# An LSTM step with its gates reordered and two gates packed in half-width products, six softmax heads moved to ScalarE, and a product lag of 4 tiles for 5

## The chip, the cores and the metric

The kernel runs on one core of one Trainium2 chip. The metric is the time of one execution on the device in microseconds, as a median of runs. The core's engines are TensorE (PE in the profile, with PEld for its weight loads), VectorE (DVE), ScalarE (ACT), GpSimd (POOL) and SyncE (SP, which issues DMAs). Each has its own instruction queue, and they meet through semaphores.

## The reference, cut to what matters

Four layers in a row, over an x of 4 x 1024 x 256 in float32. Most of the time goes to the first, a recurrence over 1024 time steps that can't be parallelised over time:

```python
def step(carry, x_t):
    h0, c0, h1, c1, a = carry
    xin = concatenate([x_t, a])
    h0, c0 = lstm_cell(xin, h0, c0, Wi0, Wh0, bi0, bh0)
    h1, c1 = lstm_cell(h0, h1, c1, Wi1, Wh1, bi1, bh1)
    q = h1 @ Wq.T
    attn = softmax(einsum('bh,bsh->bs', q, context))
    mixed = einsum('bs,bsh->bh', attn, context)
    a2 = tanh(concatenate([mixed, h1]) @ Wo.T + bo)
def lstm_cell(x, h, c, ...):      # gates i, f, g, o
    c2 = sigmoid(f) * c + sigmoid(i) * tanh(g)
    h2 = sigmoid(o) * tanh(c2)
```

After it come a quantized feed-forward layer (`gelu(x_q @ W_in_q + b_in)`, hidden width 1024), a cross-attention with 16 heads over 64 keys (`softmax(logits + mask) * group_prob @ v`), and a feed-forward layer with 8 experts. Batch is 4, the width is 256.

## The kernel before

`scan` runs the recurrence. A gate has 256 outputs. They are spread over 4 column strips of the PE array (`j`) with 64 outputs each, and the 256 inputs are cut in two (`k`), so that a gate of one product is 8 matmuls: the state (128 x 4 batch entries) is the stationary operand, 64 columns of weights are moved. A float32 matmul shows in the trace as 2 records, so a gate is 16 records and a product of four gates 64. `product(layer, state, weight, gates, done)` issues them; each layer has three PSUM banks, `F`, `IG` (gates i and g share one, in different rows) and `O`. A step has five such products: `wa` (the fed-back a, which opens the step), `wh1`, `wi1` (on the new h0), `wh0`, `wx`. It has three smaller ones too, `head_product`.

When the last product of a bank is done (`gates_summed`), DVE transposes the bank's 128x64 in blocks of 32x32 (`turn`), ACT takes tanh of it, and DVE computes 2c with one `tensor_tensor_scan` over three entries per state: it needs tanh i and tanh g, and the forget term (1 + tanh f) * c, which a separate DVE instruction (L577) makes first. Then ACT takes tanh of c (L438), keeps c (L439), and DVE makes the new h (L583), on which the next product waits. Engines take their instructions in the order in which `step` writes them.

`ffn_hidden` and `attention` run in tiles of 128 tokens with `in_steps(eng, [(stage, lag), ...])`: at step t the engine executes each stage of the list for tile t - lag, in the order of the list. In `ffn_hidden` PE runs `turn` (transposes a tile) at lag 0 and `products` at lag 5. A group is 4 tiles, whose split copies lie in `parts`, which has two buffers; ACT's `split` for a group waits until all products of the group two before are done. In `attention` (32 tiles) DVE adds the mask, takes the maximum per head, subtracts it, sums the exponentials and adds the output; ACT takes one exponential over 128x1024; GpSimd weighs; PE turns, scores, mixes and projects.

Of the kernel before, what the change touches and what calls it, by code (L numbers as in the profile page):

```python
# [12 lines left out]
AX = mybir.AxisListType  # L13
# [242 lines left out]
def scan(nc, ins, xT_all, a_hist, xres, ffn, w_out_scratch, slots_x, a_rows, w):  # L256

    U = 2
    with ExitStack() as ctx:
# [6 lines left out]
        FIRST = (B, B, 0, B)  # L266
        layer_sums = [m.psum(f"sums{l}", (P, 3, 512)) for l in range(2)]
# [3 lines left out]
        gates_of = [[turned[l][g].rearrange("p (k u) -> p k u", k=2) for g in range(3)] for l in range(2)]  # L271
        a_sumT = a_sum[:, 128:192]
# [7 lines left out]
        c = [m.sbuf(f"c{l}", [P, 2 * B]) for l in range(2)]  # L280
        forget_term = [t[:, 1].rearrange("p k b e -> p (k b) e")[:, :, 2] for t in scanned]
        ig_terms = [t[:, 0].rearrange("p k b e -> p k e b")[:, :, 1:3, :] for t in scanned]
        tanh_f = [m.sbuf(f"tanh_f{l}", [P, 2, B]) for l in range(2)]
# [12 lines left out]
        f_tanh, c_terms, c_done, c_kept, h_factors, h_ready = ([m.sem(f"{n}{l}") for l in range(2)]  # L296
                                                               for n in ("f_tanh", "c_terms", "c_done", "c_kept", "h_factors", "h_ready"))
# [20 lines left out]
        with nc.Block() as block:  # L318
# [99 lines left out]
            def _(act):  # L418
# [9 lines left out]
                def step(n):  # L428
                    for l in range(2):
                        act.wait_ge(gates_turned[l][F], n)  # L430
                        nc.scalar.activation(tanh_f[l][:], gates_of[l][F][:, :, 0:B], ACT.Tanh).then_inc(f_tanh[l], 1)  # L431
                        act.wait_ge(gates_turned[l][IG], n)
                        nc.scalar.activation(ig_terms[l], gates_of[l][IG][:, :, 0:2 * B].rearrange("p k (f b) -> p k f b", f=2),  # L433
                                             ACT.Tanh).then_inc(c_terms[l], 1)
                        act.wait_ge(gates_turned[l][O], n)
                        nc.scalar.activation(tanh_o[l][:], gates_of[l][O][:, :, 0:B], ACT.Tanh).then_inc(h_factors[l], 1)
# [1280 lines left out]
```

## Time and profile before

| | |
|---|---|
| median of 3 runs | 8204.93 us (8202.91 to 8206.75) |
| the profiled execution's own time | 8210.56 us |
| its span | 8208.8 us |
| mean granted TensorE clock | 0.984 |
| busy: PE / PEld / DVE / ACT / POOL | 85% / 72% / 55% / 42% / 4% |

The time is a little more than the span (from first to last instruction). Busy shares are means over stages with different limits. Rows of the trace name the line in the kernel, the engine, and the tiles as output<-input; `scan_sums` are the gate banks.

### The profile page before, as it was taken

The numbers are of one execution on the slowest core, as the hardware profiler recorded it, in microseconds if no ns is written. First come the engines' busy times: TensorE is split into PE (matmuls) and PEld (weight loads), VectorE is DVE, ScalarE is ACT, GpSimd is POOL, SyncE is SP. The second block draws the span as 40 slices with busy tenths as digits, with TensorE's granted clock in tenths as the row PEclk, the third lists the DMA queues.
The fourth block names the chain that finished last, engine by engine and source line by source line (L and its number), as shares of the span: only waits on it lengthen the run. The fifth ranks groups of instructions, "written<-read, shape, count | busy, mean of one in ns | idle before, by whom it ended". The sixth has DMA issues, their size and how long they took to land. (4 is left out here: it accounts for less than half of the span.)

```text
span 8208.8 us, 834179 instructions
## 1 busy us (share of the span) xinstructions
PE 6973.1 (85%) x388633; PEld 5941.0 (72%) x388641; DVE 4544.6 (55%) x21134; ACT 3446.1 (42%) x17105; POOL 312.4 (4%) x332
## 2 busy tenths in 40 slices
PE   7888888888888888888888888888888888868769
PEld 5777777777777777777777777777777777746546
DVE  5555555555555555555555555555555555566822
ACT  3444444444444444444444444444444444452422
POOL 0000000000000000000000000000000000002632
PEclk8999999999999999999999999999999999989889
DMA  3000000000000000000000000000000000000143
GB/s 113 5 0 0 5 0 0 0 0 5 0 0 0 5 0 0 0 0 5 0 0 0 5 0 0 0 5 0 0 0 0 5 0 0 0 14 11 62 148 109
DMA packets 94637, 101.99 MB, mean 12 GB/s; under 512 B 46570, under 2 KB 81904, under 8 KB 93424
## 3 DMA queue, kind: packets, MB, share of 16 engines
q1 hardware_dynamic: 89200, 88.73, 3.6%
q0 software_dynamic: 5376, 12.63, 0.4%
q14 instruction: 45, 0.37, 0.0%
q8 instruction: 16, 0.26, 0.0%
HBM read 79.75 MB, written 23.67 MB: 13 GB/s over the span
## 5 line engine op out<-in xcount | busy, mean ns | idle before, releaser
L361 PE MATMUL scan_sums<-rec_wh,scan_hT 128*4 128x64 f32 x131008 | 2394.5, 219 | 1.4 <-issue 1.3
L492 DVE STREAM_TRANSPOSE scan_sums<-scan_sums 128x64 f32<-128x64 f32 x6144 | 1551.8, 265 | 1129.8 <-PE scan_sums L361 1114.0
L361 PEld LDWEIGHTS scan_sums<-rec_wh,scan_hT 128*4 128x4 f32 x131008 | 1991.4, 89 | 2.2 <-issue 2.1
L361 PE MATMUL scan_sums<-rec_wa,scan_aT 128*4 128x64 f32 (+1 forms) x65536 | 1104.7, 219 | 474.6 <-ACT scan_aT L447 473.7
L361 PEld LDWEIGHTS scan_sums<-rec_wa,scan_aT 128*4 128x4 f32 (+1 forms) x65536 | 915.4, 88 | 663.7 <-ACT scan_aT L447 662.3
L361 PE MATMUL scan_sums<-rec_wx,scan_xT 128*4 128x64 f32 (+1 forms) x65536 | 1291.5, 219 | 3.4 <-issue 2.4
L361 PE MATMUL scan_sums<-rec_wi,scan_hT 128*4 128x64 f32 (+1 forms) x65536 | 1104.2, 219 | 145.0 <-issue 4.5
L361 PEld LDWEIGHTS scan_sums<-rec_wi,scan_hT 128*4 128x4 f32 (+1 forms) x65536 | 914.4, 88 | 334.5 <-DVE scan_hT L583 328.9
L361 PEld LDWEIGHTS scan_sums<-rec_wx,scan_xT 128*4 128x4 f32 (+1 forms) x65536 | 1023.9, 89 | 4.1 <-issue 2.9
L431 ACT ACTIVATE scan_tanh_f<-scan_sums 128x8 f32<-128x8 f32 x2048 | 364.1, 178 | 1185.9 <-DVE scan_sums L492 1185.8
L426 ACT ACTIVATE scan_sums<-rec_bias 128x192 f32<-128x192 f32 x2050 | 686.7, 335 | 303.9 <-PE scan_sums L408 6.1
L447 ACT ACTIVATE scan_aT<-scan_a_sum 128x8 f32<-128x8 f32 x1024 | 182.0, 178 | 1457.5 <-DVE scan_a_sum L598 1455.3
L372 PE MATMUL scan_scores<-rec_kp,scan_hT 128*4 128x64 f32 x16384 | 416.6, 219 | 372.6 <-DVE scan_hT L583 372.6
L372 PEld LDWEIGHTS scan_scores<-rec_kp,scan_hT 128*4 128x4 f32 x16384 | 227.6, 85 | 558.1 <-DVE scan_hT L583 558.1
L433 ACT ACTIVATE scan_scanned<-scan_sums 128x16 f32<-128x16 f32 x2048 | 393.0, 192 | 517.6 <-DVE scan_sums L492 502.1
L583 DVE SCALAR_TENSOR_TENSOR scan_hT<-scan_tanh_o,scan_sums 128x8 f32<-128x8 f32 x2048 | 335.9, 164 | 466.5 <-ACT scan_sums L438 466.0
L587 DVE TENSOR_REDUCE scan_neg_max<-scan_scores 128x1 f32<-128x65 f32 x1024 | 231.4, 226 | 517.4 <-PE scan_scores L372 517.4
L442 ACT ACTIVATE scan_exps<-scan_scores,scan_neg_max 128x64 f32<-128x64 f32 x1024 | 321.5, 314 | 430.9 <-DVE scan_neg_max L587 430.1
L581 DVE TENSOR_TENSOR_SCAN scan_sums<-scan_scanned 128x24 f32<-128x24 f32 x2048 | 443.6, 217 | 62.6 <-ACT scan_scanned L433 0.2
L372 PE MATMUL scan_a_sum<-rec_woh,scan_hT 128*4 128x64 f32 x16384 | 416.5, 219 | 0.0
L372 PE MATMUL scan_scores<-rec_vp,scan_expsT 128*4 128x64 f32 x16384 | 416.5, 219 | 0.0
L596 DVE SCALAR_TENSOR_TENSOR scan_a_natural<-scan_scores,scan_inv,scan_from_h 128x64 f32<-128x64 f32 x1024 | 290.8, 284 | 222.3 <-PE scan_scores L372 222.2
(265 smaller groups left out, 6480.6 us busy)
## 6 DMA issues: line engine op xcount, KB each, us to landing
experts_bias<-in_b SPq DMA_DIRECT2D x40, 640.0 KB, 4.3
moe_w<-in_w SPq DMA_DIRECT2D x16, 1024.0 KB, 14.7
slots_x<-scan_blank SPq DMA_DIRECT2D x40, 129.0 KB
experts_x<-slots_x SPq DMA_DIRECT2D x40, 129.0 KB
w_xres<-in_x_steps SPq DMA_DIRECT2D x8, 512.0 KB, 7.3
w_xres<-in_x SPq DMA_DIRECT2D x4, 1024.0 KB, 12.2
x_rows<-w_xres SPq DMA_DIRECT2D x4, 1024.0 KB, 8.5
a_rows<-scan_stage SPq DMA_DIRECT2D x224, 16.0 KB, 1.5
```

The costliest lines, as they stand in the source:

```text
L361: last = nc.tensor.matmul(sums[layer][BANK[g]][32 * j:32 * j + ROWS[g], 0:64], state[:, k, FIRST[g]:FIRST[g] + ROWS[g]], weight[:, k, j, 6 ...
L372: last = nc.tensor.matmul(bank[32 * j:32 * j + B, 0:64], state[:, k, :], weight[:, k, j, :], start=k == 0, stop=k == 1, skip_group_check=True)
L426: nc.scalar.activation(layer_sums[l][:, :, 0:64], w["bias"][:, l, :, :], ACT.Copy).then_inc(seeded[l], 1)
L431: nc.scalar.activation(tanh_f[l][:], gates_of[l][F][:, :, 0:B], ACT.Tanh).then_inc(f_tanh[l], 1)
L433: nc.scalar.activation(ig_terms[l], gates_of[l][IG][:, :, 0:2 * B].rearrange("p k (f b) -> p k f b", f=2), ACT.Tanh).then_inc(c_terms[l], 1)
L442: nc.scalar.activation(exps[:], scores[:, 0:S], ACT.Exp, bias=neg_max[:], accum_out=total[:]).then_inc(exps_done, 1)
L447: nc.scalar.activation(state_of(aT), a_sumT.rearrange("p (k u) -> p k u", k=2)[:, :, 0:B], ACT.Tanh).then_inc(a_ready, 1)
L492: nc.vector.transpose(turned[l][g], sums[l][g][:, 0:64]).then_inc(gates_turned[l][g], 1)
L581: nc.vector.tensor_tensor_scan(cell[l], flat[l][:, 0], flat[l][:, 1], 0.0, ALU.mult, ALU.add).then_inc(c_done[l], 1)
L583: nc.vector.scalar_tensor_tensor(state_of(hT[l]), tanh_o[l][:], 1.0, tanh_c[l].rearrange("p (k b) -> p k b", k=2), ALU.add, ALU.mult).then ...
L587: nc.vector.tensor_reduce(neg_max[:], scores[:, 0:S + 1], AX.X, ALU.max, negate=True).then_inc(max_done, 1)
L596: nc.vector.scalar_tensor_tensor(a_natural[:], mixed, inv[:], from_h[:], ALU.mult, ALU.add).then_inc(a_scaled, 1)
```

## The change

It has three parts.

1. In `scan` the gates are issued in the order i, g, f, o. Gates f and o, which used 4 rows of 64 columns, now use 8 rows of 32: each matmul of 64 columns becomes two of 32, one for each half of the strip's outputs, both summed in the same 32 columns, with the state at another row offset. DVE turns 128x32 for these two. The bias rows are laid out to match. On DVE the separate instruction now makes (1 + tanh i) * tanh g; c goes straight into the scan's operand (written there by ACT), and tanh f is written there too. The scan over three entries stays.
2. In `ffn_hidden` PE's `products` follow at lag 4.
3. In `attention` the first 6 heads (`LONE`) are taken by ACT in 6 instructions, each with the negated maximum as bias and the sum of the exponentials in `accum_out`. DVE subtracts and sums for the other 10 heads. ACT's order is turned copies, lone heads, mixed copy, exponential of the other 10. PE's next scores wait for the lone heads of the tile two before.

```diff
-                def product(layer, state, weight, gates=(GATE_F, GATE_I, GATE_G, GATE_O), done=None):
+                def product(layer, state, weight, gates=(GATE_I, GATE_G, GATE_F, GATE_O), done=None):
                     for g in gates:
-                        for k in range(2):
-                            for j in range(4):
-                                last = nc.tensor.matmul(sums[layer][BANK[g]][32 * j:32 * j + ROWS[g], 0:64],
-                                                        state[:, k, FIRST[g]:FIRST[g] + ROWS[g]],
-                                                        weight[:, k, j, 64 * g:64 * g + 64], start=False,
+                        packed = g in HALVED
+                        for half in range(2 if packed else 1):
+                            first, rows = (B * (1 - half), 2 * B) if packed else (FIRST[g], ROWS[g])
+                            width = 32 if packed else 64
+                            for k in range(2):
+                                for j in range(4):
+                                    last = nc.tensor.matmul(sums[layer][BANK[g]][32 * j:32 * j + rows, 0:width],
+                                                            state[:, k, first:first + rows],
+                                                            weight[:, k, j, 64 * g + 32 * half:64 * g + 32 * half + width], start=False,
...
                     for l in range(2):
+                        act.wait_ge(gates_turned[l][IG], n)
+                        nc.scalar.activation(tanh_ig[l][:], gates_of[l][IG][:, :, 0:2 * B].rearrange("p k (f b) -> p f k b", f=2),
+                                             ACT.Tanh).then_inc(ig_tanh[l], 1)
                         act.wait_ge(gates_turned[l][F], n)
-                        nc.scalar.activation(tanh_f[l][:], gates_of[l][F][:, :, 0:B], ACT.Tanh).then_inc(f_tanh[l], 1)
-                        act.wait_ge(gates_turned[l][IG], n)
-                        nc.scalar.activation(ig_terms[l], gates_of[l][IG][:, :, 0:2 * B].rearrange("p k (f b) -> p k f b", f=2),
-                                             ACT.Tanh).then_inc(c_terms[l], 1)
+                        nc.scalar.activation(f_factor[l], halved_of(l, F), ACT.Tanh).then_inc(c_terms[l], 1)
...
-                        nc.scalar.activation(c[l][:], twice_c[l], ACT.Copy, scale=0.5).then_inc(c_kept[l], 1)
+                        nc.scalar.activation(c_factor[l], twice_c[l], ACT.Copy, scale=0.5).then_inc(c_kept[l], 1)
...
-                    nc.vector.transpose(turned[l][g], sums[l][g][:, 0:64]).then_inc(gates_turned[l][g], 1)
+                    width = 32 if g in (F, O) else 64
+                    nc.vector.transpose(turned[l][g][:, 0:width], sums[l][g][:, 0:width]).then_inc(gates_turned[l][g], 1)
...
+                        turn(l, IG, n)
                         turn(l, F, n)
-                        turn(l, IG, n)
-                        dve.wait_ge(f_tanh[l], n)
-                        nc.vector.scalar_tensor_tensor(forget_term[l], tanh_f[l][:].rearrange("p k b -> p (k b)"), 1.0, c[l][:],
+                        dve.wait_ge(ig_tanh[l], n)
+                        nc.vector.scalar_tensor_tensor(input_term[l], tanh_ig[l][:, 0].rearrange("p k b -> p (k b)"), 1.0,
+                                                       tanh_ig[l][:, 1].rearrange("p k b -> p (k b)"),
                                                        ALU.add, ALU.mult).then_inc(c_terms[l], 1)
...
-                in_steps(pe, [(turn, 0), (products, 5)], NB // 2, 2 * B)
+                in_steps(pe, [(turn, 0), (products, 4)], NB // 2, 2 * B)
...
-                    pe.wait_ge(shifted, number(g, b))
+                    pe.wait_ge(lone_done, LONE * number(g, b))
...
+                def lone_exps(g, b):
+                    act.wait_ge(shifted, number(g, b) + 2)
+                    for h in range(LONE):
+                        nc.scalar.activation(probs[b % 2][:, h, :], heads_of[b % 2][:, h, :], ACT.Exp, bias=neg_high[b % 2][:, h:h + 1],
+                                             accum_out=total[b % 2][:, h:h + 1]).then_inc(lone_done, 1)
+
                 def exps(g, b):
-                    act.wait_ge(shifted, number(g, b) + 2)
-                    nc.scalar.activation(probs[b % 2][:], probs[b % 2][:], ACT.Exp).then_inc(exp_done, 1)
+                    nc.scalar.activation(probs[b % 2][:, LONE:H, :], probs[b % 2][:, LONE:H, :], ACT.Exp).then_inc(exp_done, 1)
...
-                in_steps(act, [(fetch, 0), (keep_turned, 3), (exps, 1), (keep_mixed, 3)])
+                in_steps(act, [(fetch, 0), (keep_turned, 3), (lone_exps, 1), (keep_mixed, 3), (exps, 1)])
...
-                    nc.vector.tensor_tensor(probs[s][:], heads_of[s], high[s][:].unsqueeze(2).broadcast_to([P, H, S]),
-                                            ALU.subtract).then_inc(shifted, 1)
+                    nc.vector.tensor_tensor(probs[s][:, LONE:H, :], heads_of[s][:, LONE:H, :],
+                                            neg_high[s][:, LONE:H].unsqueeze(2).broadcast_to([P, H - LONE, S]), ALU.add).then_inc(shifted, 1)
...
-                    nc.vector.tensor_reduce(total[b % 2][:], probs[b % 2][:], AX.X, ALU.add).then_inc(total_done, 1)
+                    nc.vector.tensor_reduce(total[b % 2][:, LONE:H], probs[b % 2][:, LONE:H, :], AX.X, ALU.add).then_inc(total_done, 1)
```

PE at the start of a time step, before: product `wa` on the fed-back a (4 or 8 stationary columns, 64 moved, xN matmuls).

```order
L361 MATMUL scan_sums<-rec_wa,scan_aT 4x64 [waits scan_a_ready]
L361 MATMUL scan_sums<-rec_wa,scan_aT 4x64 x7
L361 MATMUL scan_sums<-rec_wa,scan_aT 8x64 x16
L361 MATMUL scan_sums<-rec_wa,scan_aT 4x64 x8
L361 MATMUL scan_sums<-rec_wh,scan_hT 4x64 [waits scan_seeded1]
```

The same place in the change:

```order
L367 MATMUL scan_sums<-rec_wa,scan_aT 8x64 [waits scan_a_ready]
L367 MATMUL scan_sums<-rec_wa,scan_aT 8x64 x15
L367 MATMUL scan_sums<-rec_wa,scan_aT 8x32 x32
L367 MATMUL scan_sums<-rec_wh,scan_hT 8x64 [waits scan_seeded1]
```

Gates i and g come first, and the 8 + 8 matmuls of f and o have become 16 + 16 of half the width: 48 for 32.

DVE in one LSTM cell of layer 0, before, where `summed_f0` and its like are the PE's signals:

```order
L492 STREAM_TRANSPOSE scan_sums<-scan_sums 128x64 [waits scan_summed_f0]
L492 STREAM_TRANSPOSE scan_sums<-scan_sums 128x64 [waits scan_summed_ig0]
L577 SCALAR_TENSOR_TENSOR scan_scanned<-scan_tanh_f,scan_c 128x8 [waits scan_f_tanh0]
L492 STREAM_TRANSPOSE scan_sums<-scan_sums 128x64 [waits scan_summed_o0]
L581 SCALAR_TENSOR_TENSOR scan_sums<-scan_scanned 128x24 [waits scan_c_terms0]
```

And in the change:

```order
L499 STREAM_TRANSPOSE scan_sums<-scan_sums 128x64 [waits scan_summed_ig0]
L499 STREAM_TRANSPOSE scan_sums<-scan_sums 128x32 [waits scan_summed_f0]
L584 SCALAR_TENSOR_TENSOR scan_scanned<-scan_tanh_ig 128x8 [waits scan_ig_tanh0]
L499 STREAM_TRANSPOSE scan_sums<-scan_sums 128x32 [waits scan_summed_o0]
L589 SCALAR_TENSOR_TENSOR scan_sums<-scan_scanned 128x24 [waits scan_c_terms0]
```

The transposes have changed places, f's and o's are half as wide, and the small instruction ahead of o's transpose now waits for the tanh of i and g.

ACT in one tile of `attention` in the change, in the unrolled end of the stage (before, the two rows of L1165 were one, of 128x1024, and nothing stood behind the mixed copy):

```order
L1176 ACTIVATE ffn_hidden<-attn_turned 128x512 [waits attn_turned_done,attn_mixed_done]
L1176 ACTIVATE ffn_hidden<-attn_turned 128x512 [waits attn_turned_done]
L1165 ACTIVATE ffn_hidden<-attn_scores,ffn_hidden 128x64 [waits attn_shifted]
L1165 ACTIVATE ffn_hidden<-attn_scores,ffn_hidden 128x64 x5
L1181 ACTIVATE ffn_hidden<-attn_mixed 128x256 [waits attn_mixed_done]
L1169 ACTIVATE ffn_hidden<-ffn_hidden 128x640
```

The large exponential has become six small ones ahead of the mixed copy and a smaller one behind it.

## Rows read from the trace of the kernel before

**Rows 1.** Busy time by engine in two stretches: the scan, and the attention.

```profile
92.00:7250.00 7158.00, 6170.52 (x383986) 5394.95 (x383973) 3985.87 (x19667) 3070.14 (x16341) 20.64 (x56) 1.00 0.01 1
...
7534.00:7722.00 188.00, 138.67 (x887) 77.86 (x886) 160.90 (x184) 82.31 (x143) 124.79 (x83) 0.94 0.00 0
```

**Rows 2.** Timeline of one step: start us, duration us, engine, line, [idle before].

```profile
4001.86 1.08 PE L361 MATMUL scan_sums<-rec_wa,scan_aT 128*4 128x64 f32 x64 [0.46 <-ACT scan_aT L447]
...
4002.78 0.27 DVE L492 STREAM_TRANSPOSE scan_sums<-scan_sums 128x64 f32<-128x64 f32 x1 [0.16 <-PE scan_sums L361]
...
4002.96 0.15 DVE L577 SCALAR_TENSOR_TENSOR scan_scanned<-scan_tanh_f,scan_c 128x8 f32<-128x8 f32 x1
4003.01 0.27 DVE L492 STREAM_TRANSPOSE scan_sums<-scan_sums 128x64 f32<-128x64 f32 x1
4003.08 0.19 ACT L433 ACTIVATE scan_scanned<-scan_sums 128x16 f32<-128x16 f32 x1 [0.25 <-DVE scan_sums L492]
4003.31 0.18 ACT L436 ACTIVATE scan_tanh_o<-scan_sums 128x8 f32<-128x8 f32 x1
4003.31 0.22 DVE L581 TENSOR_TENSOR_SCAN scan_sums<-scan_scanned 128x24 f32<-128x24 f32 x1
4003.56 0.16 ACT L438 ACTIVATE scan_sums<-scan_sums 128x8 f32<-128x8 f32 x1
...
4003.97 1.08 PE L361 MATMUL scan_sums<-rec_wi,scan_hT 128*4 128x64 f32 x64
...
4008.86 0.35 PE L361 MATMUL scan_sums<-rec_wa,scan_aT 128*4 128x64 f32 x12 [0.46 <-ACT scan_aT L447]
```

**Rows 3.** Groups by shape from 3000 to 4000 us: xcount | busy us, mean ns.

```profile
L492 DVE STREAM_TRANSPOSE scan_sums<-scan_sums 128x64 f32<-128x64 f32 x858 | 215.8, 266 | 155.9 <-PE scan_sums L361 155.9
...
L591 DVE STREAM_TRANSPOSE scan_expsT<-scan_exps 128x64 f32<-128x64 f32 x142 | 34.8, 245 | 35.5 <-ACT scan_exps L442 35.5
...
L398 PE MATMUL scan_a_sum<-scan_total,w_ident 128*4 128x1 f32 x1136 | 30.6, 166 | 0.0
...
L533 DVE STREAM_TRANSPOSE scan_stage<-scan_part 128x128 f32<-128x128 f32 x8 | 2.5, 312 | 1.4 <-POOL scan_part L327 1.4
```

**Rows 4.** Timeline: ScalarE's one exponential with a sum in the scan.

```profile
4006.81 0.31 ACT L442 ACTIVATE scan_exps<-scan_scores,scan_neg_max 128x64 f32<-128x64 f32 x1 [0.42 <-DVE scan_neg_max L587]
4007.02 0.19 ACT L442 ACTIVATION_READ_ACCUMULATOR scan_exps<-scan_scores,scan_neg_max 128x1 f32 x1
```

**Rows 5.** Timeline of one attention tile: DVE, then PE, then ACT.

```profile
7604.70 1.22 DVE L1177 TENSOR_TENSOR attn_scores<-attn_scores,ffn_hidden 128x1024 f32<-128x1024 f32 x1
...
7610.36 1.22 DVE L1177 TENSOR_TENSOR attn_scores<-attn_scores,ffn_hidden 128x1024 f32<-128x1024 f32 x1
...
7606.51 1.09 PE L1118 MATMUL attn_turned<-w_ident,ffn_hidden 128*128 128x128 f32 x8 [0.47 <-POOL ffn_hidden L1216]
...
7610.59 1.10 PE L1137 MATMUL attn_y<-ffn_wo,ffn_hidden 128*128 128x256 f32 x4 [0.70 <-DVE w_xres L1198]
...
7607.20 1.09 ACT L1160 ACTIVATE ffn_hidden<-attn_turned 128x512 f32<-128x512 f32 x2 [2.35 <-PE attn_turned L1118]
...
7609.96 0.39 ACT L1165 ACTIVATE ffn_hidden<-attn_mixed 128x256 f32<-128x256 f32 x1 [0.36 <-PE attn_mixed L1128]
```

**Rows 6.** Groups by shape from 7440 to 7790 us: DVE over 1024 and 512 elements.

```profile
L1183 DVE TENSOR_TENSOR ffn_hidden<-attn_scores,ffn_hidden 128x1024 f32<-128x1024 f32 x32 | 39.2, 1225 | 3.3
...
L1060 DVE TENSOR_TENSOR ffn_hidden<-ffn_hidden 128x512 f32<-128x512 f32 x8 | 4.9, 686 | 6.0 <-ACT ffn_hidden L1019 6.0
```

**Rows 7.** PE's waits from 7280 to 7375 us: total us, times, longest.

```profile
PE hidden_turned L801 <- DVE hidden_xq L846: 21.8, 18, 1.6
```

**Rows 8.** Timeline of the hidden stage: two of PE's transposes, and a split on ACT.

```profile
7302.25 0.44 PE L801 MATMUL hidden_turned<-w_ident,hidden_xq 128*128 128x128 f32 x2 [1.61 <-DVE hidden_xq L846]
...
7313.08 0.44 PE L801 MATMUL hidden_turned<-w_ident,hidden_xq 128*128 128x128 f32 x2 [1.60 <-DVE hidden_xq L846]
...
7311.59 0.38 ACT L825 ACTIVATE hidden_parts<-hidden_turned 128x256 bf16<-128x256 f32 x1 [1.35 <-PE hidden_summed L811]
```

More of the change, by code:

```diff
@@ L279, in scan @@
         twice_c = [t.rearrange("p (v e) -> p v e", e=3)[:, :, 2] for t in cell]
[L280 to L283, printed above, removed]
+        input_term = [t[:, 1].rearrange("p k b e -> p (k b) e")[:, :, 2] for t in scanned]
+        f_factor = [t[:, 0, :, :, 1] for t in scanned]
+        c_factor = [t[:, 0].rearrange("p k b e -> p (k b) e")[:, :, 2] for t in scanned]
+        tanh_ig = [m.sbuf(f"tanh_ig{l}", [P, 2, 2, B]) for l in range(2)]
         tanh_o = [m.sbuf(f"tanh_o{l}", [P, 2, B]) for l in range(2)]
@@ L295, in scan @@
         gates_turned = [[m.sem(f"turned_{g}{l}") for g in ("f", "ig", "o")] for l in range(2)]
-        f_tanh, c_terms, c_done, c_kept, h_factors, h_ready = ([m.sem(f"{n}{l}") for l in range(2)]
-                                                               for n in ("f_tanh", "c_terms", "c_done", "c_kept", "h_factors", "h_ready"))
+        ig_tanh, c_terms, c_done, c_kept, h_factors, h_ready = ([m.sem(f"{n}{l}") for l in range(2)]
+                                                               for n in ("ig_tanh", "c_terms", "c_done", "c_kept", "h_factors", "h_ready"))
         (a_ready, x_ready, scores_done, max_done, exps_done, exps_turned, h_summed, h_kept, total_spread, a_terms, a_scaled, a_turned,
@@ L355, in _ @@
             def _(pe):
-                def product(layer, state, weight, gates=(GATE_F, GATE_I, GATE_G, GATE_O), done=None):
+                def product(layer, state, weight, gates=(GATE_I, GATE_G, GATE_F, GATE_O), done=None):
                     for g in gates:
-                        for k in range(2):
-                            for j in range(4):
-                                last = nc.tensor.matmul(sums[layer][BANK[g]][32 * j:32 * j + ROWS[g], 0:64],
-                                                        state[:, k, FIRST[g]:FIRST[g] + ROWS[g]],
-                                                        weight[:, k, j, 64 * g:64 * g + 64], start=False,
-                                                        stop=done is not None and g != GATE_I and k == 1, skip_group_check=True)
+                        packed = g in HALVED
[7 more added lines that the diff above has]
+                                                            weight[:, k, j, 64 * g + 32 * half:64 * g + 32 * half + width], start=False,
+                                                            stop=done is not None and g != GATE_I and k == 1 and (half == 1 or not packed),
+                                                            skip_group_check=True)
                         if done is not None and g != GATE_I:
@@ L1084, in attention @@
         mixedT = [m.sbuf(f"mixedT{i}", [P, KC, P]) for i in range(2)]
-        high, total, inv = (([m.sbuf(f"{n}{i}", [P, H]) for i in range(2)]) for n in ("high", "total", "inv"))
+        LONE = 6
+        neg_high, total, inv = (([m.sbuf(f"{n}{i}", [P, H]) for i in range(2)]) for n in ("neg_high", "total", "inv"))
         scores = [m.psum(f"scores{i}", (P, KC, 512)) for i in range(2)]
@@ L1669, in bias_rows @@
         rows = np.zeros((4, 32, GATES, 64), bias.dtype)
-        for g, first in enumerate((0, 0, B, 0)):
-            rows[:, first:first + B, g, :] = gate_blocks(bias)[g][:, None, :]
+        blocks = gate_blocks(bias)
+        for g, first in ((1, 0), (2, B)):
+            rows[:, first:first + B, g, :] = blocks[g][:, None, :]
+        for g in (0, 3):
+            for half in range(2):
+                rows[:, B * half:B * half + B, g, 0:32] = blocks[g][:, None, 32 * half:32 * half + 32]
         return rows.reshape(P, GATES, 64)
```

11 lines of the change are left out of this document (7 added, 4 removed).

## The prediction, made before the changed kernel was run

> **What bounds the kernel now.** I read the busy time by stretches first: the scan takes 7158 of 8209 us [rows 1], so a change of 0.01 us in a time step is worth 10 us. PE is busy 86% of it, which looks like the bound, but the timeline of one step says otherwise. A step lasts 7.00 us (4001.86 to 4008.86), and PE opens it after 0.46 us of waiting for `scan_aT` [rows 2]. The end is set by a ring of short dependent instructions: PE, transpose, tanh, scan, tanh, h, PE, twice per step, and then the attention part. PE's other products fill its waits.
>
> Follow cell 0 [rows 2]. PE starts `wa` at 4001.86. The transpose of bank IG starts at 4002.78, 0.92 after it, and takes 0.266 us [rows 3]. ACT's tanh of IG runs 4003.08 to 4003.27, the scan starts at 4003.31, tanh of c at 4003.56, the next product at 4003.97. The reader is to see that IG, the second bank, is on the path, and that o's transpose (4003.01 to 4003.28) ends at almost the same moment, so both have to get earlier. From the start of `wa` to the scan it is 1.45 us.
>
> **The scan, part by part.** First the pitch of PE. The 64 records of `wa` last 1.08 us and one lasts 0.219, so the starts spread over 0.861 us [rows 2] (one with a single column lasts 0.166 [rows 3]). The four column strips run side by side, so this is 16 groups of 4 records. I take 0.02 us for the starts within a group and get (0.861 - 0.02) / 15 = 0.056 us from group to group. What a group of 32 columns needs, no row shows. Bounds: if only the columns count, 0.028. If nothing is saved, 0.056. The nearest row is the spread of totals with one column, 8 records (2 groups): 1136 records are 142 steps, 30.6 / 142 = 0.2155 us each, less 0.166 is 0.0495, less 0.02 leaves 0.03 for the second group [rows 3]. I take 0.031, as 32 columns can't be quicker than one, and call it P.
>
> The end of a matmul moves too: 64 columns take 0.219, one takes 0.166 [rows 2, 3], so 32 take about 0.192, 0.027 less.
>
> Path through the second bank, now f: before, the last group of IG started 11 x 0.056 = 0.613 after the first and the transpose 0.92 after it, an offset of 0.307. Now it is 8 x 0.056 + 7 x 0.031 = 0.663, and 0.663 + 0.307 - 0.027 = 0.943. The transpose is 128x32. From 64 to 128 columns it goes from 0.245 to 0.312 us [rows 3], so 32 columns less are 0.033 less: 0.233. Handing over to ACT takes 0.03 (4003.05 to 4003.08), tanh over 8 elements 0.178 where 16 took 0.19 (rows of 4003.31 and 4003.08), and handing over to DVE 0.03 to 0.04 [rows 2]. Sum: 0.943 + 0.233 + 0.033 + 0.178 + 0.032 = 1.42, where the same sum for IG gives 0.92 + 0.266 + 0.033 + 0.19 + 0.032 = 1.44. **0.026 us less.**
>
> Path through the new wait of DVE on `ig_tanh`: behind it on DVE stand o's transpose and the scan. IG now is summed after 7 groups: 0.92 - 0.613 + 0.39 = 0.70; + 0.266 + 0.033 + 0.19 + 0.032 = 1.22 for the small instruction; o's transpose can start 0.05 later (4002.96 to 4003.01), and behind a transpose of 64 columns the next instruction starts 0.18 later (4002.78 to 4002.96) [rows 2], so behind 32 about 0.14: the scan at 1.41. That is just under the other path. Bank O is summed for 0.448 + 15 x 0.031 + 0.28 = 1.19, before 1.27: not late. tanh of o ends at 1.27 + 0.23 + 0.03 + 0.18 = 1.71, before tanh of c would (1.42 + 0.22 + 0.03 + 0.16 = 1.83): hidden. With P = 0.028 the f path gives 1.40 and DVE's 1.41 decides: 0.034 us less. With P = 0.0347 the gain is nil (0.026 / 7 more). Both cells are alike (`wi1` starts at 4003.97 after the same ring), so a step gains 0.052 us: **53 us** over 1024 steps (70 at P = 0.028).
>
> PE's load: a product takes 8 x 0.056 + 16 x 0.031 = 0.94 where it took 0.89. `wa` and `wh1` end at 4001.86 + 1.88 = 4003.74, ahead of 4003.97: hidden. The exponential is read out at 4007.21 [rows 4] while PE, delayed by two packed gates (0.05), finishes about there. It costs nothing, and without that cover up to 0.05 us a step (50 us). ACT's copy of c and the seeds only write elsewhere: nothing.
>
> **Attention.** One tile takes 5.66 us (7604.70 to 7610.36) [rows 5], and DVE is busy 161 of the stage's 188 us [rows 1]. 1024 elements take 1.225 us, 512 take 0.686 [rows 6]: 1.05 ns an element. Subtraction and sum each lose 384: 0.40 us each, so DVE would allow 4.86. But a new ring appears: PE turns, ACT copies 0.69 later (7606.51 to 7607.20), two copies 0.99, six heads, mixed copy 0.39, PE projects (1.10, of which 0.87 until the next can start) and turns the next tile [rows 5], since the mixed copy now stands behind the lone heads. A head: the read of the sum starts 0.21 behind the exponential and lasts 0.19 [rows 4]. Bounds 0.28 and 0.40 a head; I take 0.34, as ACT's instructions overlap by some 0.1 us. Ring: 0.69 + 0.99 + 6 x 0.34 + 0.39 + 0.06 + 0.87 = 5.04 us. The tile gains 0.62 (0.26 at 0.40 a head, 0.80 at 0.28 where DVE decides). Times 31 tiles: **19 us** (8 to 25).
>
> **Hidden stage.** A group of 4 tiles takes 10.83 us (7302.25 to 7313.08), and PE waits 1.6 us in each at one tile, where ACT's split waits for PE's products of the group two before [rows 8]. With lag 5 these stand behind the turn of the tile that needs the buffer. With lag 4 they stand ahead of it, so that wait goes. The stage has 8 groups; six such waits are 10 us. All 18 waits add up to 21.8 us [rows 7], of which 12 lie in the start, where the products now begin one tile sooner, and in shorter waits behind the long one. Of these I take a third: **14 us** in all (8 to 16). The products need the tile whose low part DVE made before the turn ahead of them: no new wait.
>
> **Sum.** 53 + 19 + 14 = 86 us of the profiled 8210.6: 8124.6. The median of the runs is 5.6 us lower than that execution, so 8204.9 - 86 = 8119 us.
>
> **A rule of the skill against it.** The spread shows four matmuls of one column started in about 0.05 us [rows 3], 0.013 each, and a float32 matmul of 64 columns now costs 0.056 / 2 = 0.028 of PE's time. The Trainium skill, TensorE: Matmul & The Clock Gate, section "Wait — 56ns, not 53.3ns?", says that start-to-start never drops below about 25 ns, however few columns. By that rule a matmul of 32 columns would save next to nothing, and rival 2 would be the result. The one-column row speaks against it across strips, but it is a burst of four behind a wait, not a stream of 48.
>
> **Rivals.**
> 1. P is 0.034 to 0.037: the scan gains nothing (8172 by the 33 us of the other stages) or gives back as much as they bring (at 0.037, 0.0023 x 7 x 2048 = 33 us, 8205). For it: the P of the one-column row comes from two groups with 4 stationary columns, not 8. Chance 0.14.
> 2. Slower: issue sets PE's pace, not columns. Its place is f and o in `wa` and `wi1`, its price for P = 0.050 (a matmul no cheaper than 0.025 us): bank O's last group starts at 0.448 + 15 x 0.05 = 1.20, its transpose at 1.48, the scan at 1.62 to 1.65, 0.2 us later in each cell: 410 us, less 33: 8580. It decides from P = 0.038 on. For it: 188 matmuls a step are now 268. Against it: the one-column row. Chance 0.12.
> 3. More: a transpose of 32 columns takes 0.21 and frees DVE after 0.12, P = 0.028. Then f's path is 1.375 and DVE's 1.39: 0.055 less in each cell, 113 us, with 19 to 40 from the others: 8060. For it: a 128x8 instruction takes only 0.15 [rows 2]. Chance 0.14.
>
> **Chances and range.** The forecast, 8119, 0.60 (its own range 8090 to 8160). A measurement of this kernel tells 0.2%, 16 us, from no change. Faster: 0.60 + 0.14 + half of rival 1, less 0.02 for what I don't see: 0.79. Within 0.2%: 0.08. Slower: 0.13. Rival 2 stays outside, as do the ends of the others: 8052 to 8208.
>
> **What would show it.** In the profile after: the groups of 128x32 matmuls, whose 32 records per gate spread over 8P (0.25 us; 0.40 means rival 2); the transpose of f at 0.94 after `wa` starts, of 0.23 us; the scan at 1.42; steps of 6.95 us; PE's waits on `scan_aT` still there. In attention DVE's add every 5.0 us with PE's projection waiting on ACT's mixed copy. In the hidden stage groups of 8.7 to 9.3 us. It is wrong if a strip's weight load with 8 stationary columns can't be renewed in 0.03 us, or if two halves that add to the same PSUM columns hold each other up.

## The result

The changed kernel took 8238.53 us (median of 5 runs, 8236.22 to 8241.55), the kernel before 8204.93 (8202.25 to 8207.31, 5 runs beside them): a ratio of 1.004, interval 1.0027 to 1.0054. It is slower by 34 us where 86 less were forecast. Two of the three parts brought what was forecast or more; the third, which carried most of the sum, has the wrong sign.

The page of the kernel after: span, busy time of TensorE (PE) and of its weight loads (PEld), and the granted clock in 40 slices.

```profile
span 8234.5 us, 1162182 instructions
...
PE 7411.6 (90%) x552448; PEld 6680.3 (81%) x552449; DVE 4494.4 (55%) x21132; ACT 3459.2 (42%) x17489; POOL 312.4 (4%) x332
...
PEclk8999999999999999999999999999999999999889
```

Before, the same page has 388633 records of PE in 6973.1 us. So 42% more matmul records, and PE busy for 438 us more. The clock row differs in one slice alone, behind the scan (9 where 8 stood before), and in the scan the granted clock is 1.00 in both kernels: the 2.4 GHz level, so the scan's difference doesn't come from there.

Busy time by engine in the scan of the kernel after (stretch, length, then each engine's busy time and records; to be set beside [rows 1]).

```profile
92.00:7317.00 7225.00, 6621.45 (x547637) 6138.50 (x547629) 3964.58 (x19675) 3048.89 (x16346) 20.57 (x56) 1.00 0.01 1
```

Where the time went is read from the first start of one line in each stage, before and after:

| first start of | before | after | shift |
|---|---|---|---|
| the scan's products | 61.5 | 59.9 | -1.6 |
| (last `wh` product of the scan) | 7247.5 | 7314.8 | +67.3 |
| hidden stage, turning | 7278.8 | 7346.8 | +68.0 |
| `output_summed` | 7386.2 | 7440.0 | +53.8 |
| attention, DVE's add | 7560.8 | 7613.9 | +53.1 |
| routing, turning | 7759.6 | 7786.3 | +26.7 |
| end of the span | 8208.8 | 8234.5 | +25.7 |

The scan lost 69 us, the hidden stage gave back 14 and attention 26. (Between the spans lie 26 us, between the medians 34.)

One time step of the kernel after, in the timeline (start us, duration us; to be set beside [rows 2]).

```profile
4004.68 1.20 PE L367 MATMUL scan_sums<-rec_wa,scan_aT 128*8 128x64 f32 x96 [0.42 <-ACT scan_aT L454]
...
4005.38 0.53 DVE L499 STREAM_TRANSPOSE scan_sums<-scan_sums 128x64 f32<-128x64 f32 x2 [0.44 <-PE scan_sums L367]
4005.68 0.19 ACT L438 ACTIVATE scan_tanh_ig<-scan_sums 128x16 f32<-128x16 f32 x1 [0.85 <-DVE scan_sums L499]
...
4005.70 1.17 PE L367 MATMUL scan_sums<-rec_wh,scan_hT 128*8 128x64 f32 x96
4005.90 0.17 DVE L584 SCALAR_TENSOR_TENSOR scan_scanned<-scan_tanh_ig 128x8 f32<-128x8 f32 x1
4005.94 0.18 ACT L441 ACTIVATE scan_scanned<-scan_sums 128x8 f32<-128x8 f32 x1
4005.99 0.23 DVE L499 STREAM_TRANSPOSE scan_sums<-scan_sums 128x32 f32<-128x32 f32 x1
4006.16 0.22 DVE L589 TENSOR_TENSOR_SCAN scan_sums<-scan_scanned 128x24 f32<-128x24 f32 x1
...
4006.41 0.16 ACT L445 ACTIVATE scan_sums<-scan_sums 128x8 f32<-128x8 f32 x1
...
4006.82 1.20 PE L367 MATMUL scan_sums<-rec_wi,scan_hT 128*8 128x64 f32 x96
```

The two transposes in one row are IG's (64 columns) and f's (32); f's takes the last 0.23 of the 0.53, so it starts at 4005.68, 1.00 after `wa`, where 0.94 was forecast. ACT's tanh of f (L441) starts at 4005.94, 0.26 later, and the scan at 4006.16: 1.48 after `wa`, where 1.42 was forecast and 1.45 was read before. The 96 records of `wa` last 1.20 us and one of 32 columns 0.193 (below), so the starts spread over 1.01 us where 0.93 was forecast (0.913 to the last group and 0.02 within it).

Groups by shape of the kernel after from 3000 to 4000 us (busy us, mean ns; to be set beside [rows 3]).

```profile
L367 PE MATMUL scan_sums<-rec_wa,scan_aT 128*8 128x32 f32 x9088 | 106.1, 193 | 0.0
...
L499 DVE STREAM_TRANSPOSE scan_sums<-scan_sums 128x32 f32<-128x32 f32 x566 | 129.0, 228 | 7.7
...
L367 PE MATMUL scan_sums<-rec_wa,scan_aT 128*8 128x64 f32 x4544 | 89.9, 219 | 59.4 <-ACT scan_aT L454 59.4
L499 DVE STREAM_TRANSPOSE scan_sums<-scan_sums 128x64 f32<-128x64 f32 x283 | 75.1, 265 | 167.3 <-PE scan_sums L367 167.3
...
L584 DVE SCALAR_TENSOR_TENSOR scan_scanned<-scan_tanh_ig 128x8 f32<-128x8 f32 x283 | 48.8, 172 | 0.2 <-ACT scan_tanh_ig L438 0.2
```

The durations of single instructions were forecast well: 0.193 for 0.192, 0.228 for 0.233. What was not is how closely the matmuls follow each other.

The starts of the single records of `wa` show it (ns; 230 is the first one; two records a matmul, eight to a line). In every step from 3000 to 3800 us the closely spaced starts end at the same record, the first of the 13th matmul.

```
after, gate g, last lines (64 columns)     569  575  582  589   625  631  638  645
after, gate f (2 x 32 columns)             680  687  694  700   709  715  722  729
                                           738  745  751  758   767  774  780  787
                                           796  803  810  816   825  832  839  845
                                           855  879  884  895   909  912  925  946
after, gate o                              955  971  985  988  1001 1005 1017 1021 ... 1217 1239
16-column kernel (e5), gate f              679  686  693  700   708  715  721  728
                                           733  740  747  753   759  765  771  779
                                           783  790  797  804   809  815  822  829
                                           834  871  879  895   909  912  924  946
16-column kernel, gate o                   954  971  984  988  1002 1005 1017 1022 ... 1217 1239
```

Groups of four records come every 56 ns with 64 columns. With 32 they come every 29 ns, as forecast, but only from 680 to 855, for 12 matmuls; with 16 every 26 ns, for the same 12. Behind them there is a matmul (two records) every 16.6 ns, with 32 columns and with 16: 33 ns for a group of four. f's last record starts 0.717 us behind the first (a median of 0.716) where 0.683 was forecast (0.663 for the last group and 0.02 within it), o's at 1.009.

### The profile page after: what moved, and what is told of

Read it like the earlier page. It is cut to its first block and busy times, and to the rows that moved or that the text cites. A ratio compares the mean times of both kernels' runs of the same rounds, so it can differ in the third digit from the quotient of the medians.

```text
span 8234.5 us, 1162182 instructions
## 1 busy us (share of the span) xinstructions
PE 7411.6 (90%) x552448; PEld 6680.3 (81%) x552449; DVE 4494.4 (55%) x21132; ACT 3459.2 (42%) x17489; POOL 312.4 (4%) x332
## 5 line engine op out<-in xcount | busy, mean ns | idle before, releaser
L367 PE MATMUL scan_sums<-rec_wh,scan_hT 128*8 128x64 f32 (+1 forms) x196512 | 2640.6, 202 | 7.3 <-issue 7.3
L367 PEld LDWEIGHTS scan_sums<-rec_wh,scan_hT 128*8 128x8 f32 x196512 | 2249.8, 89 | 7.8 <-issue 7.8
L499 DVE STREAM_TRANSPOSE scan_sums<-scan_sums 128x32 f32<-128x32 f32 (+1 forms) x6144 | 1475.2, 240 | 1285.3 <-PE scan_sums L367 1229.3
L367 PE MATMUL scan_sums<-rec_wa,scan_aT 128*8 128x64 f32 (+1 forms) x98304 | 1227.9, 202 | 426.4 <-ACT scan_aT L454 426.2
L367 PEld LDWEIGHTS scan_sums<-rec_wa,scan_aT 128*8 128x8 f32 x98304 | 1095.3, 89 | 557.7 <-ACT scan_aT L454 557.3
L367 PE MATMUL scan_sums<-rec_wx,scan_xT 128*8 128x64 f32 (+1 forms) x98304 | 1416.8, 202 | 3.3 <-issue 2.5
L367 PE MATMUL scan_sums<-rec_wi,scan_hT 128*8 128x64 f32 (+1 forms) x98304 | 1228.2, 202 | 5.7 <-issue 5.3
L367 PEld LDWEIGHTS scan_sums<-rec_wi,scan_hT 128*8 128x8 f32 x98304 | 1095.4, 89 | 88.2 <-issue 5.6
L367 PEld LDWEIGHTS scan_sums<-rec_wx,scan_xT 128*8 128x8 f32 x98304 | 1155.6, 89 | 3.9 <-issue 2.7
L438 ACT ACTIVATE scan_tanh_ig<-scan_sums 128x16 f32<-128x16 f32 x2048 | 377.7, 184 | 1619.8 <-DVE scan_sums L499 1619.8
L441 ACT ACTIVATE scan_scanned<-scan_sums 128x8 f32<-128x8 f32 x2048 | 373.9, 183 | 154.8 <-DVE scan_sums L499 2.2
```

The lines of the kernel that those rows point to most:

```text
L438: nc.scalar.activation(tanh_ig[l][:], gates_of[l][IG][:, :, 0:2 * B].rearrange("p k (f b) -> p f k b", f=2), ACT.Tanh).then_inc(ig_tanh[l], 1)
L441: nc.scalar.activation(f_factor[l], halved_of(l, F), ACT.Tanh).then_inc(c_terms[l], 1)
L499: nc.vector.transpose(turned[l][g][:, 0:width], sums[l][g][:, 0:width]).then_inc(gates_turned[l][g], 1)
```

## The experiments

Times are medians. Of kernels timed in rounds the interval of the ratio is given; the kernel before took 8205.52 beside e1 to e4, 8203.55 beside e5 to e7 and 8205.6 beside e8 to e11. Times within a step are medians over 3000 to 3800 us, counted from the first start of `wa`.

| us after `wa` starts | before | after | e2 | e3 | e4 | e5 | e6 | e7 |
|---|---|---|---|---|---|---|---|---|
| last start of f's matmuls | .188 | .716 | .638 | .638 | .716 | .717 | .717 | .557 |
| transpose of f starts | .474 | .994 | .924 | .924 | .993 | .993 | .994 | .875 |
| tanh ends | 1.412 | 1.441 | 1.405 | 1.405 | 1.439 | 1.439 | 1.441 | 1.308 |
| transpose of o starts | 1.144 | 1.301 | 1.300 | 1.300 | 1.299 | 1.300 | 1.300 | 1.299 |
| scan starts | 1.444 | 1.475 | 1.466 | 1.437 | 1.472 | 1.472 | 1.473 | 1.432 |
| scan ends | 1.661 | 1.692 | 1.653 | 1.653 | 1.689 | 1.689 | 1.690 | 1.636 |
| step | 7.000 | 7.067 | 6.989 | 6.988 | 7.058 | 7.058 | 7.066 | 6.955 |

(The tanh is that of i and g in the kernel before, of f in the others. The scan's end is what tanh of c, and so the rest of the ring, waits for.)

**e1, the scan of before with the two other parts.**

```diff
-                def product(layer, state, weight, gates=(GATE_I, GATE_G, GATE_F, GATE_O), done=None):
+                def product(layer, state, weight, gates=(GATE_F, GATE_I, GATE_G, GATE_O), done=None):
...
```

> The scan of the kernel before with the change's hidden and attention stages. By the traces the scan of the changed kernel is 69 us longer (a step 7.067 for 7.000 us), the hidden stage 14 us and the attention 26 us shorter. Theory (all of the loss lies in the scan): 8205 - 41 = 8164 us. Rival (the scan's loss is partly put down wrongly and the later stages gave less): above 8180.

Measured: 8164.9, ratio 0.995 (0.9937 to 0.9964). The attention and hidden parts bring 41 us together; the loss is the scan's alone. The diffs that follow leave out lines that only fit the kernel to the edit (the bias rows, the views of the turned gates).

**e2, the new order of gates without packing.**

```diff
-        HALVED = (GATE_F, GATE_O)
+        HALVED = ()
...
-                    width = 32 if g in (F, O) else 64
+                    width = 64
```

> The change without the packing: gates in the order i, g, f, o, all 64 columns wide, 32 matmuls a product. Theory A (PE can't issue a float32 matmul faster than one in 16.6 ns, so the 32 halves run dry and f and o are summed 0.03 and 0.08 us late): step 6.99 to 7.00 us, 8155 to 8166 us. Theory B (the new order itself costs: DVE's small instruction now waits for tanh of i and g, two transposes stand back to back): the step stays at 7.06 us, 8225 to 8240 us.

Measured: 8151.84, ratio 0.9933 (0.992 to 0.9947), 13 us below e1 and the fastest of the kernels that compute the whole layer (e3's and e10's intervals overlap its own). Its timeline of one step:

```profile
3999.87 1.08 PE L367 MATMUL scan_sums<-rec_wa,scan_aT 128*8 128x64 f32 x64 [0.47 <-ACT scan_aT L454]
...
4000.57 0.49 DVE L499 STREAM_TRANSPOSE scan_sums<-scan_sums 128x64 f32<-128x64 f32 x2 [0.44 <-PE scan_sums L367]
...
4001.09 0.17 DVE L584 SCALAR_TENSOR_TENSOR scan_scanned<-scan_tanh_ig 128x8 f32<-128x8 f32 x1
4001.09 0.18 ACT L441 ACTIVATE scan_scanned<-scan_sums 128x8 f32<-128x8 f32 x1
4001.17 0.26 DVE L499 STREAM_TRANSPOSE scan_sums<-scan_sums 128x64 f32<-128x64 f32 x1
4001.34 0.19 DVE L589 TENSOR_TENSOR_SCAN scan_sums<-scan_scanned 128x24 f32<-128x24 f32 x1
...
4006.86 1.08 PE L367 MATMUL scan_sums<-rec_wa,scan_aT 128*8 128x64 f32 x64 [0.47 <-ACT scan_aT L454]
```

The tanh of f starts at 4001.09, 1.22 after `wa`; with packing it was 1.26. The step is 6.989 for 7.000 before: the order gains 0.011 us a step, 11 of the 13 us, and the theory that the order or its new wait costs the time falls: the loss comes with the packing.

**e3 and e4, only one gate packed.**

```diff
-        HALVED = (GATE_F, GATE_O)
+        HALVED = (GATE_O,)        (e3)
+        HALVED = (GATE_F,)        (e4)
```

> Order i, g, f, o, only o packed. Theory A: f is summed after 12 groups as IG was before; o is summed in time behind the small instruction: scan of a cell 1.44 us after the product starts, step 7.00 us, 8158 to 8170 us. Theory B: 8225 to 8240 us.

> Order i, g, f, o, only f packed. Theory A: f's last matmul is as late as in the changed kernel (0.72 us after the product's start, for 0.63 unpacked), its narrower transpose and shorter matmul give back 0.06 of the 0.08: step 7.05 to 7.06 us, 8220 to 8238 us. If the late o alone is at fault: 8165 us.

Measured: e3 8157.94 (0.9941, 0.9926 to 0.9956), its step 6.988, as in e2; e4 8229.84 (1.003, 1.0019 to 1.0042). Of the 87 us between e2 and the changed kernel, 78 come with f. In e4's timeline:

```profile
4002.39 0.17 DVE L584 SCALAR_TENSOR_TENSOR scan_scanned<-scan_tanh_ig 128x8 f32<-128x8 f32 x1
4002.43 0.18 ACT L441 ACTIVATE scan_scanned<-scan_sums 128x8 f32<-128x8 f32 x1
4002.47 0.26 DVE L499 STREAM_TRANSPOSE scan_sums<-scan_sums 128x64 f32<-128x64 f32 x1
4002.64 0.22 DVE L589 TENSOR_TENSOR_SCAN scan_sums<-scan_scanned 128x24 f32<-128x24 f32 x1
```

Here the small DVE instruction (L584) and o's transpose stand against each other as in e2, but tanh of f starts 0.04 behind the first of them instead of beside it, and the scan follows it. In e3 the scan starts 0.03 earlier than in e2 but is drawn 0.22 long for 0.19: it ends at 1.653 in both, 0.248 behind the end of the tanh of f. So the scan's start is a poor measure, and its end hangs on f; a narrower transpose of o buys nothing. In e3 the burst is seen once more: o's 16 matmuls come behind 24 of 64 columns instead of 16, and again 12 of them come at 14.6 ns each, with a gap of 24 ns behind them. So the burst doesn't get longer with more matmuls ahead of it, and it isn't tied to gate f.

**e5, e6 and e7: why the packed matmuls are slow.** Three kernels vary one thing each in the packed gates of the changed kernel: moved columns, stationary columns (`rows` in the code, 8 or 4), and count. None of them computes the layer: e5 leaves out half of what f and o sum, e6 adds both halves into the same rows, and e7 leaves the second halves out.

```diff
# e5: moved columns
-    sums[layer][BANK[g]][32 * j:32 * j + rows, 0:width]
+    sums[layer][BANK[g]][32 * j:32 * j + rows, 0:width // 2 if packed else width]
...
# e6: stationary columns
-    first, rows = (B * (1 - half), 2 * B) if packed else (FIRST[g], ROWS[g])
+    first, rows = (B, B) if packed else (FIRST[g], ROWS[g])
# e7: count
-    for half in range(2 if packed else 1):
+    for half in range(1):
...
```

> The changed kernel with the packed matmuls cut to 16 moved columns (half of what gates f and o sum is left out); as many matmuls. Theory A (issue): once PE has used up what was issued ahead, one float32 matmul still takes 16.6 ns, so bank O's last matmul starts only 0.0 to 0.05 us earlier than the 1.01 us after wa's first, and a step stays at 7.02 to 7.06 us. Rival C (columns and their turnaround set the pace of the halves): twice as quick, O's last matmul at 0.8 us.

> The changed kernel with 4 stationary columns for 8 in the packed halves (each half then adds into the same rows, so f and o are wrong sums); as many matmuls of 32 columns. Theory A (issue): pace and step unchanged, 16.6 ns and 7.06 us. Rival D (the load of 8 stationary columns can't be renewed in 0.03 us): the pace falls to 14.5 ns or less and the step to 7.03 us or less.

> The changed kernel with the second halves of f and o left out: 32 matmuls a product, half of them of 32 columns. Theory A: f is summed early enough for its transpose to stand right behind IG's, and what is left is DVE's and ACT's own chain through tanh of i and g: scan 1.42 to 1.45 us after wa starts, step 6.96 to 6.99 us. If the step stays above 7.04 the matmuls aren't at fault.

Measured, one run each: 8231.34, 8242.14 and 8122.49. Half the columns change little (a step of 7.058 for 7.067): e5's `wa` and `wh1` still start 1.02 apart, as in the changed kernel (4004.68, 4005.70), and the list of starts above runs into the same times from 879 on.

```profile
4003.72 1.19 PE L367 MATMUL scan_sums<-rec_wa,scan_aT 128*8 128x64 f32 x96 [0.43 <-ACT scan_aT L454]
4004.74 1.15 PE L367 MATMUL scan_sums<-rec_wh,scan_hT 128*8 128x64 f32 x96
4005.86 1.19 PE L367 MATMUL scan_sums<-rec_wi,scan_hT 128*8 128x64 f32 x96
```

In e6 tanh of f stands 1.26 behind `wa` and the scan 1.48, and the starts of `wa` lie within 2 ns of the changed kernel's: the eight stationary columns are not it either.

```profile
4000.95 1.20 PE L367 MATMUL scan_sums<-rec_wa,scan_aT 128*8 128x64 f32 x96 [0.42 <-ACT scan_aT L454]
...
4002.21 0.18 ACT L441 ACTIVATE scan_scanned<-scan_sums 128x8 f32<-128x8 f32 x1
...
4002.43 0.22 DVE L589 TENSOR_TENSOR_SCAN scan_sums<-scan_scanned 128x24 f32<-128x24 f32 x1
```

Only the count moves it. In e7 the packed gates have as many matmuls as unpacked ones, and as many moved columns in all as in e5, where there are twice as many matmuls:

```profile
4002.55 0.91 PE L367 MATMUL scan_sums<-rec_wa,scan_aT 128*8 128x64 f32 x64 [0.57 <-ACT scan_aT L454]
...
4003.67 0.18 ACT L441 ACTIVATE scan_scanned<-scan_sums 128x8 f32<-128x8 f32 x1
4003.76 0.17 DVE L584 SCALAR_TENSOR_TENSOR scan_scanned<-scan_tanh_ig 128x8 f32<-128x8 f32 x1
4003.85 0.23 DVE L499 STREAM_TRANSPOSE scan_sums<-scan_sums 128x32 f32<-128x32 f32 x1
4003.98 0.20 DVE L589 TENSOR_TENSOR_SCAN scan_sums<-scan_scanned 128x24 f32<-128x24 f32 x1
```

It shows a second thing. f is out of the way here (its tanh ends at 1.308), yet the scan starts at 1.432: L584 waits for the tanh of i and g (which ends at 1.18 in every kernel with the new order) and starts at 1.22, the next instruction starts 0.084 behind it and the scan 0.133 behind o's transpose. That is a floor that no speed of f gets under; the forecast had the start at 1.41. The scan ends at 1.636 here, 0.017 before e2's. So 0.034 us a step, 35 us in all, is what a quicker f can still gain on e2 in this order, and this kernel gains it with half of f's and o's work left out.

**e8 and e9, the other two parts alone on the kernel before.**

```diff
# e8
-                in_steps(pe, [(turn, 0), (products, 5)], NB // 2, 2 * B)
+                in_steps(pe, [(turn, 0), (products, 4)], NB // 2, 2 * B)
# e9: the attention part of the change, whole
+        LONE = 6
...
```

> The kernel before with products at lag 4 only. By the traces of before and after the hidden stage (first transpose to the next stage's first product) goes from 107.4 to 93.2 us: 14 us less, 8191 us. Rival: the stages behind hide or give back part of it: 8200 us.

> The kernel before with the new attention only. By the traces the stage (DVE's first add to the next stage's first transpose) goes from 198.8 to 172.4 us: 26 us less, 8179 us.

Measured: 8188.71 (0.9981, 0.9972 to 0.999), 17 us less, and 8179.89 (0.9969, 0.9957 to 0.9981), 26 less. In the changed kernel, PE's waits for the tiles to turn (before, in [rows 7]: 21.8 us, 18 times) and two turns four tiles apart (before, in [rows 8]):

```profile
PE hidden_turned L809 <- DVE hidden_xq L854: 6.7, 5, 1.6
```

```profile
7364.73 0.44 PE L809 MATMUL hidden_turned<-w_ident,hidden_xq 128*128 128x128 f32 x2 [0.34 <-DVE hidden_xq L854]
...
7373.44 0.44 PE L809 MATMUL hidden_turned<-w_ident,hidden_xq 128*128 128x128 f32 x2
```

Four tiles take 8.71 us where they took 10.83. One attention tile of the changed kernel (to be set beside [rows 5]):

```profile
7633.72 1.23 DVE L1193 TENSOR_TENSOR attn_scores<-attn_scores,ffn_hidden 128x1024 f32<-128x1024 f32 x1
...
7634.62 1.13 PE L1148 MATMUL attn_y<-ffn_wo,ffn_hidden 128*128 128x256 f32 x4 [0.51 <-ACT ffn_hidden L1181]
...
7637.20 0.32 ACT L1165 ACTIVATE ffn_hidden<-attn_scores,ffn_hidden 128x64 f32<-128x64 f32 x1
7637.40 0.21 ACT L1165 ACTIVATION_READ_ACCUMULATOR ffn_hidden<-attn_scores,ffn_hidden 128x1 f32 x1
7637.49 0.33 ACT L1165 ACTIVATE ffn_hidden<-attn_scores,ffn_hidden 128x64 f32<-128x64 f32 x1
...
7638.59 1.22 DVE L1193 TENSOR_TENSOR attn_scores<-attn_scores,ffn_hidden 128x1024 f32<-128x1024 f32 x1
```

A head takes 0.29 us (7637.20 to 7637.49): the next exponential starts 0.09 after the read of the sum begins. The tile takes 4.87, and DVE starts its add without a wait: DVE sets it, not the ring.

**e10 and e11, five and seven lone heads, in e2's kernel.**

```diff
-        LONE = 6
+        LONE = 5        (e10)
+        LONE = 7        (e11)
```

> The order without the packing, with 5 lone heads for 6. DVE sets the attention tile (4.87 us with 6 heads; each head back on DVE costs 2 x 64 elements x 1.05 ns = 0.13 us): 5.00 us a tile, 4 us in all slower than the 8152 of 6 heads: 8156 us. If the ring over ACT sets the tile, it gets shorter by 0.29 instead: 8150 us or less.

> The same with 7 lone heads. DVE would allow 4.74 us; the ring PE turns, ACT copies, lone heads at 0.29 us each, mixed copy, PE projects is 0.69 + 0.99 + 7 x 0.29 + 0.39 + 0.06 + 0.87 = 5.03 us: 5 us in all slower, 8157 us. If DVE alone counts: 8148 us.

Measured: 8157.68 (0.9942, 0.9929 to 0.9956) and 8161.31 (0.9947, 0.9933 to 0.9961). Against the kernel before beside each that is 48 and 44 us less, where six heads (e2) gave 54; the intervals overlap. The tiles tell them apart: a median of 4.86 with six, 4.99 with five (DVE has 64 elements more in two instructions), 5.09 with seven, where DVE's add waits for PE's scores. These don't wait themselves: they stand on PE behind the projection (L1148), which waits for ACT's mixed copy (L1181), and that stands on ACT behind the seven lone heads. It is the ring of the prediction, expected at 5.03:

```profile
7609.86 1.23 DVE L1193 TENSOR_TENSOR attn_scores<-attn_scores,ffn_hidden 128x1024 f32<-128x1024 f32 x1 [0.34 <-PE attn_scores L1118]
7614.94 1.23 DVE L1193 TENSOR_TENSOR attn_scores<-attn_scores,ffn_hidden 128x1024 f32<-128x1024 f32 x1 [0.26 <-PE attn_scores L1118]
...
7611.07 1.13 PE L1148 MATMUL attn_y<-ffn_wo,ffn_hidden 128*128 128x256 f32 x4 [0.79 <-ACT ffn_hidden L1181]
7612.03 1.04 PE L1129 MATMUL attn_turned<-w_ident,ffn_hidden 128*128 128x128 f32 x8
7612.91 1.88 PE L1118 MATMUL attn_scores<-ffn_hidden 128*128 128x512 f32 x4
```

The best version is e2: the new order, the hidden and the attention part, and no packing.

## Why the prediction was wrong

**What bounds the kernel: right.** The step is set by the ring of short instructions through the second bank. The scan starts 0.031 us later in each cell (1.475 for 1.444); two cells make 0.062 of the 0.067 us by which the step grew, and 1024 steps make the 69 us. The scan's end moves by as much (1.692 for 1.661). That PE's other products are hidden held too: PE still waits 0.42 us for `scan_aT` before `wa`. The last 0.005 us of the step are not accounted for.

**The pitch P, 0.031: the step that failed.** It was taken from two groups of four records and laid over the 16 groups of gates f and o. The runs show two regimes. A burst comes at the pace of the columns, 0.029 a group at 32, and for that the one-column row was a fair guide. After 12 matmuls the burst is used up, and matmuls start 16.6 ns apart, with 32 columns and with 16 (e5), with eight stationary columns and with four (e6). 0.033 a group is in itself near P, and by the prediction's sum would leave a small gain of about 0.01 us a cell. But the change of regime costs more than the pitches tell: from 855 to 946 there are seven starts, where the burst has some 12. So f's last start came 0.034 late (0.717 for 0.683). That is the larger part of the 0.055 by which the scan started late (1.475 for 1.42).

**The shorter end of a narrower matmul, 0.027: mis-sized.** It was taken from drawn durations (0.219 and 0.192). Behind a last start with 64 columns the transpose follows after 0.287 (0.634 to 0.921 for IG before, and within 0.001 in e2 for f), with 32 columns after 0.277, and with 16 (e5) after 0.277 too. So 0.010 was gained where 0.027 was put, and f's transpose started at 0.994 for 0.943. The other terms of that path (0.233, 0.033, 0.178, 0.032) are right within 0.005 each.

**The sum itself has a slip.** Its own terms give 1.419 for the path through f and 1.441 for the one through IG, 0.022 less and not 0.026: 45 us and not 53. (8 x 0.056 + 7 x 0.031 is 0.665, not 0.663, and 11 x 0.056 is 0.616, not 0.613; these two nearly cancel.)

**The path through the new wait, 1.41: too short by the start, near by the end.** L584 starts at 1.217, as forecast (1.22). What stands behind it starts 0.084 later, where 0.05 was taken from another instruction, so by this path the scan starts at 1.43 (e7: 1.432). But it is drawn 0.204 long there for 0.217 before, and ends at 1.636 for 1.661: 0.025 less in each cell, 51 us. So this path alone would have let most of the forecast through, and e7 shows it: 0.045 us a step less than before.

**What a right pitch would have brought.** The scan ends 0.248 behind the tanh of f in e2, e3 and the changed kernel (within 0.003). With f's starts as forecast its tanh would have ended at 1.441 - 0.034 = 1.407, as in e2, and the scan at 1.655: an estimate of 0.006 a cell, 12 us, and not 53. Had the burst's 0.029 lasted over the whole gate, the last start would be at 0.448 + 7 x 0.029 + 0.02 = 0.671 and the scan's end at 1.643: an estimate of 0.018 a cell, 37 us. No run shows either. What the packing lost against e2 is the pitch; what it could have won was small unless the burst had lasted.

**Bank O in time: wrong in time, harmless.** o's last record starts at 1.009 for 0.933 forecast, but its transpose stands behind L584 on DVE until 1.30 anyway; e3 shows it free.

**Rival 2, issue sets PE's pace:** the mechanism is the one that came, its place and price are not. It put the loss in bank O at 0.2 us a cell (410 us); it lies in f at 0.03. Its floor of 0.050 a group was too high: the groups came every 0.033. The Trainium skill, TensorE: Matmul & The Clock Gate, section "Wait — 56ns, not 53.3ns?", says that start-to-start never drops below about 25 ns. The trace doesn't agree with that figure for matmuls in different column strips, which start 14.6 ns apart in the burst and 16.6 after it, but it agrees that narrower matmuls stop paying: behind the burst, 16 columns are no quicker than 32.

**Attention, -19: too small.** By the stages it is 26.4 us, by e9 25.7. A head takes 0.29 for the 0.34 taken, near the lower bound of 0.28, and there DVE's 4.86 decides, as the prediction said it would: 4.87. **Hidden stage, -14: right** (14.2 by the stages, 16.9 by e8), with 8.71 a group at the lower end of the forecast 8.7 to 9.3, and 15 of the 21.8 us of waits gone.

What stays open: what feeds the burst. That the loss depends on the number of matmuls and not on their moved (32 or 16) or stationary columns (8 or 4) is shown, though e5, e6 and e7 are single runs (their step times are medians over 113 steps or more). Each matmul brings its own weight loads, and no run changes the number of loads without that of matmuls, so a fixed cost of a load is not told apart from one of the matmul or of its instruction. Nor does a run show why the burst is 12 matmuls long, or why the first start behind it comes 24 ns (32 columns) or 37 ns (16 columns) after the one before.

## What to carry to other kernels

Cutting a matmul into two of half the columns halved the pitch here for the first 12 matmuls and no longer: count the matmuls behind the wait, and ask for the pitch of a stream as long as the one you build, not of the first groups of one. When one input of a join is sped up, work out the other inputs and the queue of the joining engine just as closely, because they cap what the speed-up can bring (here at 0.017 us a cell beyond the new order). Measure at the end of the joined instruction: its drawn start moved by 0.03 us (e2 to e3) with nothing gained. Where one of several parts fails, run the parts alone: without the packing (e2) the kernel is 54 us below the one before and 87 below the changed one. 41 of the 54 come from the attention and hidden parts, the rest from the new order.

## What the runs showed of the hardware

- Float32 matmuls with eight stationary columns in four column strips start 28 ns apart at 64 columns. Behind a stream of these the first 12 narrower ones start 14.6 ns apart at 32 columns and 12.9 at 16 (after, e3, e5, e7); then it is 16.6 ns each with either width (after, e5).
- The transpose that waits for a bank starts 0.287 us behind the start of the last matmul record of 64 columns and 0.277 behind one of 32 or 16 columns, though the drawn durations differ by more (0.219 and 0.193).
- The next DVE instruction starts 0.166 to 0.174 us behind a transpose of 128x64 from PSUM (e2, before) and 0.133 behind one of 128x32 (e7), but 0.084 behind the small instruction that reads two parts of one tile (0.172 us long), where it was 0.05 behind the one before (0.153).
- On ACT, exponentials over 128x64 that also sum follow each other every 0.29 us (after), though each is drawn 0.32 to 0.36 long with a read of 0.21 to 0.25 behind it: the drawn durations of such pairs overlap and can't be added.
